# The router's normal rows and constants made beside the first attention, its affine step on ACT, its logits in two banks

## What is computed

```python
x = x + (o @ wo + bo)
hn2 = _layernorm(x, ln2_g, ln2_b).reshape(-1, h)
logits = hn2 @ gate_w + gate_b
idx = jnp.argmax(logits, axis=-1)
mid = jax.nn.relu(jnp.einsum('th,ehf->etf', hn2, w1) + b1[:, None, :])
y = jnp.einsum('etf,efh->eth', mid, w2) + b2[:, None, :]
moe = y[idx, jnp.arange(hn2.shape[0])]
return x + moe.reshape(b, s, h)
```

## Time and profile before

| | us |
|---|---|
| median of three runs | 2004.15 |
| the profiled execution | 2003.47 |
| its span in the trace | 2001.8 |
| first attention, first maxima's product to last residual | 331.27 to 709.41 |
| router, first constant to first load of sorted rows | 710.71 to 779.19 |
| busy over the span: TensorE, VectorE, ACT, POOL | 1750.6, 1582.9, 1286.3, 1103.4 |

### The profile page before, as it was taken

One profiled execution on the slowest core, in us unless ns is written; L12 is line 12 of the kernel. 1 busy time (PEld: TensorE's weight loads), 2 busy tenths in 40 slices (PEclk: granted clock), 3 DMA queues, 4 the chain that ended last, 5 costly groups with the idle time before them and its releaser, 6 DMA issues. The chain is left out here.

```text
span 2001.8 us, 48064 instructions
## 1 busy us (share of the span) xinstructions
PE 1750.6 (87%) x18438; PEld 754.1 (38%) x18438; DVE 1582.9 (79%) x2988; ACT 1286.3 (64%) x2656; POOL 1103.4 (55%) x712
## 2 busy tenths in 40 slices
PE   5537857999999955977999999999999999999997
PEld 3337832233333344653442333333333333333333
DVE  7853567999999565437879999989989899998963
ACT  4503243888888810216884777777887877787785
POOL 8713541000000056331134888989899998989895
PEclk9769977899999956998997999999999999999998
DMA  1230045111111061127994232332323223232311
GB/s 48 36 51 3 1 139 196 49 45 44 49 40 49 13 199 50 50 58 259 373 405 139 69 86 71 80 81 70 86 65 86 75 76 85 66 87 68 82 29 42
DMA packets 194488, 180.14 MB, mean 90 GB/s; under 512 B 58741, under 2 KB 155125, under 8 KB 194053
## 3 DMA queue, kind: packets, MB, share of 16 engines
q1 hardware_dynamic: 185860, 170.01, 29.1%
q0 software_dynamic: 2944, 7.10, 1.1%
q10 hardware_dynamic: 5504, 0.73, 0.2%
HBM read 101.16 MB, written 75.26 MB: 88 GB/s over the span
## 5 line engine op out<-in xcount | busy, mean ns | idle before, releaser
L1037 ACT ACTIVATE probs_l<-exp_l 128x512 f32<-128x512 f32 x1024 | 575.4, 595 | 197.3 <-PE exp_l L1088 189.4
L951 POOL TENSOR_TENSOR part_sums_l<-probs_l 128x1024 f32<-128x1024 f32 x256 | 604.3, 2361 | 110.7 <-ACT probs_l L1037 99.5
L975 DVE TENSOR_REDUCE maxima_l<-max_l 128x1 f32<-128x512 f32 x1024 | 634.0, 682 | 35.5 <-PE max_l L1077 35.5
L1077 PE MATMUL max_l<-k_stack_l,q_stack_l 96*128 96x512 f16 x1024 | 399.7, 391 | 4.0 <-DVE pv_bank_l L967 3.3
L1088 PE MATMUL exp_l<-q_stack_l,k_stack_l 100*128 100x512 f16 x1024 | 390.1, 382 | 5.3 <-ACT probs_l L1037 2.9
L1279 DVE TENSOR_REDUCE maxima_l<-max_l 128x1 f32<-128x512 f32 x512 | 317.1, 683 | 16.6 <-PE max_l L1365 16.5
L1316 ACT ACTIVATE probs_l<-exp_l 128x512 f32<-128x512 f32 x512 | 279.2, 600 | 58.3 <-PE exp_l L1378 54.6
L1122 PE MATMUL pv_bank_l<-probs_l,v_ring_l 128*32 128x512 f32 x2048 | 274.5, 608 | 0.5 <-ACT probs_l L1037 0.5
L1077 PEld LDWEIGHTS max_l<-k_stack_l,q_stack_l 96*128 96x128 f16 x1024 | 100.3, 98 | 328.1 <-DVE maxima_l L975 286.2
L1793 POOL IOTA rows_e<- 128x32 int32 x1 | 0.2, 183 | 384.6 <-POOLq L26 384.6
L957 POOL TENSOR_TENSOR part_sums_l<-part_sums_l 128x512 f32<-128x512 f32 x128 | 163.0, 1273 | 10.0
(11 more groups left out here) (294 smaller groups left out, 2474.8 us busy)
## 6 DMA issues: line engine op xcount, KB each, us to landing
scratch_qk_l<-parts_g SPq DMA_DIRECT2D x128, 256.0 KB, 9.1
q_stack_l<-scratch_qk_l SPq DMA_DIRECT2D x192, 128.0 KB
k_stack_l<-scratch_qk_l SPq DMA_DIRECT2D x192, 128.0 KB
scratch_v_l<-v_g SPq DMA_DIRECT2D x16, 1024.0 KB
v_ring_l<-scratch_v_l SPq DMA_DIRECT2D x64, 256.0 KB, 3.3
scratch_stack_l<-parts_c SPq DMA_DIRECT2D x16, 384.0 KB, 3.8
q_stack_l<-scratch_stack_l SPq DMA_DIRECT2D x64, 96.0 KB, 2.2
k_stack_l<-scratch_stack_l SPq DMA_DIRECT2D x64, 96.0 KB, 2.3
```

Source lines behind the costliest of these rows:

```text
L951: pool.tensor_tensor(part_sums[:, i, h, :, :], probs[:, i, h, 0:2, :], probs[:, i, h, 2:4, :], ALU.add).then_inc(pair_sum.sem, 1)
L975: dve.reduce_max(maxima[:, s % 2, at % NT, at // NT:at // NT + 1], max_bank(n, at)[:, :], AX).then_inc(max_taken.sem, 1)
L1037: act.activation(probs[:, i, at // NT, at % NT, :], exp_ps[at % 2][:, :], ACT.Exp, scale=a.scale).then_inc(prob_tile.sem, 1)
L1077: pe.matmul(max_bank(n, at)[:, :], qs[0:SHIFT_ROW, s % RING, h, k * P:(k + 1) * P], ks[0:SHIFT_ROW, s % RING, h, :], start=True, stop=True ...
```

## The change

- `open_router` allocates the router's rows, constants and gate tensors ahead of `prep_l0`, so that they live through the attention.
- In `attention_l0` SP first issues the four small loads of the gate. POOL makes all constants at the block's start. ACT does, for batch `b` in turn `b + 2`, four sums of 128x128 in group s=1 (one after tile 3, two after tile 9, one after tile 11) and four sums of squares at the same places of group s=2. POOL makes 1/std and the normal rows of the batch from them. This covers batches 0 to 6.
- In `moe` only batch 7 has its moments and normal rows taken as before. The affine step goes from VectorE to ACT. The logits use two banks (those of the experts' first product), so the scores of a batch wait for the choice two before. TensorE transposes two batches ahead and scores one ahead. VectorE's order is: moments 7, choice 0, normal rows 7, destinations 0, choice 1, then choice b and destinations b-1. POOL does one power and then its 32 stores without anything between. ACT does the eight affine steps, then its fills, then the next layer's weights (which stood ahead of the fills).

The core of the diff:

```diff
+ROW_SUMS_AT = {(1, 3): (0,), (1, 9): (1, 2), (1, 11): (3,)}
+ROW_SQUARES_AT = {(2, 3): (0,), (2, 9): (1, 2), (2, 11): (3,)}
...
@@ attention_l0, pool
+            for b in range(ROWS_BESIDE):
+                tiles = slice(b * NT, (b + 1) * NT)
+                pool.wait_ge(row_squared.sem, row_squared.made(b, NT - 1))
+                did(pool.tensor_scalar(rstd[:, tiles], squares[:, tiles], 1.0 / D, None, ALU.mult))
+                settle()
+                did(pool.tensor_scalar(rstd[:, tiles], rstd[:, tiles], LN_EPS, None, ALU.add))
+                settle()
+                did(pool.tensor_tensor(rstd[:, tiles], rstd[:, tiles], g.minus_half[:, 0:NT], ALU.pow))
+                did(pool.tensor_tensor(r.rows[:, tiles, 0:D], g.z[:, tiles, :], bc(minus_mean[:, tiles], D), ALU.add))
+                settle()
+                did(pool.tensor_tensor(r.rows[:, tiles, 0:D], r.rows[:, tiles, 0:D], bc(rstd[:, tiles], D), ALU.mult))
+            settle()
...
@@ attention_l0, act
+            def moments_beside(turn, s, at):
+                b = turn - 2
+                if not 0 <= b < ROWS_BESIDE:
+                    return
+                for k in ROW_SUMS_AT.get((s, at), ()):
+                    tile = b * NT + k
+                    if k == 0:
+
+                        act.wait_ge(y_taken.sem, b + 1)
+                    act.activation(junk[:, k, :], g.z[:, tile, :], ACT.Identity, scale=-1.0 / D,
+                                   accum_out=minus_mean[:, tile:tile + 1]).then_inc(row_summed.sem, 1)
+                for k in ROW_SQUARES_AT.get((s, at), ()):
+                    tile = b * NT + k
+                    act.wait_ge(row_summed.sem, row_summed.made(b, NT - 1))
+                    act.activation(junk[:, k, :], g.z[:, tile, :], ACT.Square, bias=minus_mean[:, tile:tile + 1],
+                                   accum_out=squares[:, tile:tile + 1]).then_inc(row_squared.sem, 1)
...
@@ moe, pool
-            for i in range(B + 2):
-                if i < B:
-                    reciprocal_std(i)
-                if i >= 2:
-                    scatter(i - 2)
+            for b in range(B):
+                scatter(b)
...
@@ moe, vector
-            for i in range(B + 2):
-                if i < B:
-                    take_moments(i)
-                if 1 <= i <= B:
-                    affine(i - 1)
-                if i >= 2:
-                    destine(i - 2)
-                if i < B:
-                    normalise(i)
-                if 1 <= i <= B:
-                    choose(i - 1)
+            take_moments(last_b)
+            choose(0)
+            normalise(last_b)
+            destine(0)
+            choose(1)
+            for b in range(2, B):
+                choose(b)
+                destine(b - 1)
+            destine(B - 1)
             tabulate()
...
@@ moe, scalar
-            act.wait_ge(zeros_ready, 2)
+            for b in range(B):
+                act.wait_ge(zT_ps.sem, zT_ps.made(b, 0))
+                act.activation(hT[:, b % 2, :], zT_bank[b % 2][:, :], ACT.Identity, bias=col[:, 1:2], scale=col[:, 0:1]).then_inc(hT_ready.sem, 1)
+            fill_tails(act, range(E_ // 2, E_))
             act.wait_ge(w_qkv_loaded, 16)
             act.mul(w_qkv[:, :], w_qkv[:, :], W_SCALE).then_inc(w_scaled, 1)
...
@@ moe, tensor
                 pe.wait_ge(hT_ready.sem, hT_ready.made(b, 0))
-                if b:
-                    pe.wait_ge(chosen.sem, chosen.made(b - 1, 0))
+                if b >= 2:
+                    pe.wait_ge(chosen.sem, chosen.made(b - 2, 0))
...
+            transposes(0)
+            transposes(1)
+            score(0)
+            for b in range(B):
+                if b + 2 < B:
+                    transposes(b + 2)
+                if b + 1 < B:
+                    score(b + 1)
+                rank(b)
```

More of the change, by code:

```diff
@@ L1183, with open_router, attention_l0 @@
 L0_OT_AT, L0_OUT_AT = 7, 7
-def attention_l0(nc, g, scratch):
+E_, F_ = 8, 512
+FT = F_ // P
+ROUTES = T + E_
+REGION = B * N + P
+ROW = D + 1
+ROWS_BESIDE = B - 1
+ROW_SUMS_AT = {(1, 3): (0,), (1, 9): (1, 2), (1, 11): (3,)}
+ROW_SQUARES_AT = {(2, 3): (0,), (2, 9): (1, 2), (2, 11): (3,)}
+def open_router(nc, g, ctx):
+    sb = lambda name, shape, dt=F32: ctx.enter_context(nc.sbuf_tensor(name + "_router", shape, dt))
+    r = g.router = Shared()
+    r.gate_w, r.gate_b, r.col = sb("gate_w", [P, E_]), sb("gate_b", [P, E_]), sb("col", [P, 2])
+    r.rows, r.zeros = sb("rows", [P, T, ROW]), sb("zeros", [P, 2 * E_, ROW])
+    r.below, r.ones = sb("below", [P, P]), sb("ones", [P, P])
+    r.pref, r.region, r.upto = sb("pref", [P, NT, E_]), sb("region", [P, E_]), sb("upto", [P, E_, E_])
+    r.steps, r.routes = sb("steps", [P, T]), sb("routes", [P, ROUTES])
+def attention_l0(nc, g, ins, scratch):
     a = L0_ATT
@@ L1202, in attention_l0 @@
         inv_sums, o, oT = sb("inv_sums", [P, NT, HG]), sb("o", [P, NT, U, HG, W]), sb("oT", [P, N])
+        junk = sb("junk", [P, NT, D])
+        minus_mean, squares, rstd = [sb(name, [P, T]) for name in ("minus_mean", "squares", "rstd")]
         cleared = sem("cleared")
@@ L1230, in _ @@
         @block.sync
         def _(sp):
+            sp.dma_start(g.router.gate_w[:, :], ins["L0_ffn_gate_w"]).then_inc(gate_loaded, 16)
+            sp.dma_start(g.router.gate_b[:, :], ins["L0_ffn_gate_b"].partition_broadcast(P)).then_inc(gate_loaded, 16)
+            for n, name in enumerate(("ln2_g", "ln2_b")):
+                sp.dma_start(g.router.col[:, n:n + 1], ins["L0_ffn_" + name].rearrange("(p a) -> p a", a=1)).then_inc(gate_loaded, 16)
             for i in range(2):
@@ L1709, in moe @@
         midT_bank, y_bank = [pb(f"midT{i}") for i in range(2)], [pb(f"y{i}") for i in range(2)]
-        logits_bank, rank_bank = y_bank
+        logits_bank, rank_bank = mid_bank, y_bank[1]
+        r, last_b = g.router, B - 1
         w1, w2 = sb("w1", [P, E_, F_]), sb("w2", [P, E_, FT, D])
         b1, b2 = sb("b1", [P, E_, F_]), sb("b2", [P, E_, D])
[L1713 to L1720, removed]
+        gate_w, gate_b, col, rows, zeros = r.gate_w, r.gate_b, r.col, r.rows, r.zeros
+        below, ones, pref, region, upto, steps, routes = r.below, r.ones, r.pref, r.region, r.upto, r.steps, r.routes
+        stats, mv = sb("stats", [P, NT, 6]), sb("mv", [P, NT, 2])
+        var_eps, rstd = sb("var_eps", [P, NT]), sb("rstd", [P, NT])
         hT = sb("hT", [P, 2, N])
@@ L1791, in _ @@
         def _(pool):
[L1793 to L1815, removed]
+            pool.wait_ge(moments, 1)
+            pool.tensor_tensor(rstd[:, :], var_eps[:, :], g.minus_half[:, 0:NT], ALU.pow).then_inc(rstd_ready, 1)
             def scatter(b):
@@ L1909, in tabulate @@
                 dve.wait_ge(counted, 1)
[L1910 removed]
+                did(dve.tensor_copy(count[:, :], logits_bank[0][:, 0:E_]))
                 settle()
@@ L2032, in rank @@
                 pe.matmul(rank_bank[:, 0:NT * E_], ones[:, :], before[:, at, :], start=False, stop=True).then_inc(rank_ps.sem, 1)
-            for i in range(B + 1):
-                if i >= 1:
-                    score(i - 1)
-                if i < B:
-                    transposes(i)
-                if i >= 1:
-                    rank(i - 1)
-            pe.matmul(logits_bank[:, 0:E_], ones[:, :], before[:, T, :], start=True, stop=True).then_inc(counted, 1)
+            transposes(0)
[7 more added lines that the diff above has]
+                rank(b)
+            pe.matmul(logits_bank[0][:, 0:E_], ones[:, :], before[:, T, :], start=True, stop=True).then_inc(counted, 1)
             pe.wait_ge(experts_in, 64)
```

79 lines of the change are left out of this document (43 added, 36 removed).

## The result

Over four executions the changed kernel took a median of 1986.27 us (1983.01 to 1988.09), the kernel before 2003.31 beside it. The ratio is 0.9906 [0.9894, 0.9919], or 18.8 us off 2003.31 [16.2, 21.2], which puts the changed kernel at 1984.5. The kernel became faster by the forecast's mechanism, and by more than the forecast of 15.2 us: 1984.5 lies 0.5 us under the range's lower end of 1985.0, with an interval of its own from 1982.1 to 1987.1. A repeat gave 0.9904 [0.9890, 0.9917], 1983.8 against 2003.02; one of its six executions took 5528 us, is taken for a slow one and stands in no figure here.

What follows compares the result with a forecast made beforehand. The prediction took POOL's stores to become the router's bound; the router's -15.9 us and the attention drain's +0.7 made -15.2, from 2003.47 to 1988.3 us, with a range of 1985.0 to 1996.5.

Steps and rivals of the forecast that it cites:

- the sum: Whole kernel: router -15.9 us and attention's drain +0.7 make -15.2, from 2003.47 to 1988.3 us.
- The landing: Router's end: from the last store's end to the first load of sorted rows, 1.4 us, at most 5.2.
- The bound: Router: POOL's 32 stores become the bound, with choices running ahead, at a pace of 1.29 us a store.
- Rival 1: Router: stores keep their old pace of 1.47 us, a gain of 10.9 us, 1993.3 in all; chance 0.15.
- The first store: Router's start, built up step by step: first store at 720.3, 7.1 us earlier than 727.39.
- The stores' length: Router: 31 x 1.29 + 1.0 = 41.0 us, plus 0.6 for stores beside big weight loads, 41.6.
- Rival 2: Router's end: another landing is late, 5.2 us behind the last store instead of 1.4, 1992.1; chance 0.06.
- Steady turns at nothing: First attention: ACT's added sums and squares fit its waiting and cost 0 us in the steady turns.
- The drain's 0.7: First attention's last turn: the sums of batch 6 show among ACT's nine exponentials, costing 0.7 us.
- rival 5: Router's start: POOL ends batch 6's rows behind the residual, needing 1.5 us over the upper estimate; chance counted in spread.
- Rival 3: First attention: reads of ACT's accumulators don't overlap, 10.5 us more, 1998.8; chance 0.05.
- Rival 4: First attention: ACT becomes the bound, kernel slower, 2017.6 us; decides from 15.9 us, 2.3 a turn; chance 0.05.

Runs made afterwards that it cites:

- idle powers: Changed kernel with seven unused 128x4 powers put back on POOL, one ahead of each batch's stores but the first; router 59.33 us, 7.1 more.
- the long row: Changed kernel with rows of the sorted table of 640 bytes instead of 516, stored and loaded whole; router 51.74 us, landing 2.07.

## Where the prediction failed, and what of it held

**The step that failed** is the sum, in three of its terms: the router's gain of 15.9 us was made of a first store 10.9 us behind the residual (9.70 measured) and stores of 41.6 us (40.27 measured), each too long, and the attention's drain was charged 0.7 us that it didn't cost. The landing erred the other way (1.4 for 2.22) and hid 0.8 of this, by luck. So the router gave 17.6 us and the attention took nothing, 17.6 together instead of 15.2. The mechanism, POOL's queue as the bound, held.

**The bound.** Right. POOL's stores set the router, with choices running ahead (idle powers: 7.1 us for 7.3). Rival 1, the old pace, is out: 40.27 us for 32 stores, 1.27 apart. The Trainium skill, SBUF — State Buffer, section SBUF: two separate sides, tells of a lock: while a two-port instruction of VectorE runs, POOL can't write its descriptors, which would stretch the stores. Most last 0.95 to 0.96 beside VectorE's small steps; the mean is 963 ns, and 997 with the rows in the router. Little of that difference can be such a lock's: in that run too a store lasts 0.95 to 0.98 unless it is the next behind a power (1.09 to 1.11), but for two of 1.11 and 1.19 near the end that no run explains. Behind the idle powers, with no rows on VectorE, it is 1.04. An estimate from these: the rows on VectorE lengthen five stores by some 0.06, 0.3 us in all.

**The first store.** The mechanism was right, the term too large: 10.9 us behind the residual forecast, 9.70 measured. The clock has no part in this difference: the rows that I took stand at a granted clock of 0.50 (718 to 726 us), as the new start does. Counted from the residual, the transposes of both batches ended at 3.3 us (forecast 3.8; eight took 1.94 on end), the scores of batch 0 at 5.2 (5.7), its choice at 7.3 (7.9) and its rank at 8.5 (9.8). Half a microsecond is the transposes, and 0.7 is at the rank: I had set transposes 2 and scores 1 end to end before it, but each starts as the piece before still runs, its weights being loaded beside, and they kept the rank off only to 718.30, 0.15 behind the choice.

**The stores' length.** 41.6 forecast, 40.27 measured. The mean of before, 0.992, held six stores next behind a power (1.03 to 1.17), of which the change left one, and two long ones near the end; and I added 0.6 for the weight loads besides, though only the first two stores (1.12, 0.98) are longer. The gap between the old pace of 1.47 and 1.29 I had put down to eight powers, which would be 8.3 us over a difference of 31 x 0.18 = 5.6; five stood there, 5.2. The sum doesn't use that reading. At 0.96 and 0.30 it is 31 x 1.26 + 0.96 = 40.0.

**The landing.** 1.4 forecast, 2.22 measured: the likeliest end was too small, since SP's reading of the address was left out, as far as the rows tell. Rival 2's 5.2 is out: the fills had landed.

**The attention.** Steady turns at nothing: right, to 0.01 us. The drain's 0.7 was wrong. ACT around the sums of batch 6, answering to the earlier trace rows:

```profile
691.96 1.59 ACT L1403 ACTIVATE probs_l<-exp_l 128x512 f32<-128x512 f32 x3
693.40 0.34 ACT L1383 ACTIVATE junk_l<-z_res 128x128 f32<-128x128 f32 x1
693.60 0.23 ACT L1383 ACTIVATION_READ_ACCUMULATOR junk_l<-z_res 128x1 f32 x1
693.69 3.07 ACT L1403 ACTIVATE probs_l<-exp_l 128x512 f32<-128x512 f32 x6
696.64 0.32 ACT L1383 ACTIVATE junk_l<-z_res 128x128 f32<-128x128 f32 x1
...
697.23 1.09 ACT L1403 ACTIVATE probs_l<-exp_l 128x512 f32<-128x512 f32 x2
...
705.44 1.04 POOL L1292 TENSOR_TENSOR rows_router<-rows_router,rstd_l 128x512 f32<-128x512 f32 x1
...
710.13 0.69 DVE L1366 TENSOR_TENSOR z_res<-misc_l,z_res 128x512 f32<-128x512 f32 x1 [2.58 <-PE misc_l L1495]
```

The two exponentials behind the gap start at 697.23, 1.41 later than at 695.82, of which 1.4 is the attention's later start. The nine exponentials that the earlier trace rows merges (4.71 us for nine) weren't on end: the third and fourth of them start 0.70 apart, the others 0.48 to 0.50, and the first sum took that place. POOL's rows of batch 6 were done at 706.48, 4.3 us before the residual: rival 5 is out.

**Rival 3**, the reads not overlapping: out, 0.38 us from square to square. No further table load: the attention has one, as before. **Rival 4** was given the right mechanism and the wrong point. Its 15.9 us, 2.3 a turn, treated the slack as one account. It is one for each group, some 1.4 us and what three banks carry, and the change's 1.56 us of squares just fit; twice that costs 0.9 us a turn at full clock, and 11.0 over the attention with what the clock adds.

**What was not priced.** I costed the exchange of the affine step at nothing and the second bank not at all. Undone alone they cost 1.85 and 3.2 us, both through the first two batches. And the 3.45 us of VectorE's wait for the constants, which I read as part of the old start, cost next to nothing when the constants alone went back. That this did no harm is owed to the new start's being built up from its steps and not as old start less parts.

**The range.** Its lower end lay 3.3 us under the forecast, where the terms of the sum were each taken at the likeliest or a cautious value: 1.2 for the start, 1.3 for the stores, 0.7 for the drain, less 0.8 for the landing, 2.4 together. The ratio puts the time another 1.4 lower; in the repeat's trace, where the clock fell later, the router is 1.1 shorter still. The upper side had rivals, the lower had none, though two rows (a mean over mixed surroundings, engines set end to end) could only err to that side.

## What to carry to other kernels

When a stage is bounded by one queue, price the rest of it only until that queue is full: a second bank, or an engine's step moved away, counts during the fill and nowhere later. Slack has to be read in the stretch in which the moved work must end, between the events that hand buffers on, and not as a share of a turn. Work that fills a gap to the last tenth was free here; the same again cost 0.05 us in one group and 0.8 in the next, and only the run could tell.

## What the runs showed of the hardware

**The clock at a stage's edge.** The same instructions of the changed kernel took different time at the router's start. Busy time and granted clock (third figure from the end) in 712 to 716 us, first after, then its repeat:

```profile
712.00:716.00 4.00, 3.83 (x17) 3.46 (x18) 1.42 (x10) 1.56 (x2) 1.02 (x1) 0.50 0.58 149
```
```profile
712.00:716.00 4.00, 3.57 (x24) 3.33 (x23) 2.54 (x17) 2.23 (x3) 1.02 (x1) 0.74 0.70 208
```

At 0.50 TensorE runs at 1.2 GHz, at 1.00 at 2.4. After the change the clock fell at 711.1, ahead of the first product at 712.15; in the repeat only at 713.9, and the first store came 1.24 us earlier (8.46 against 9.70). The eight transposes and the eight first score products took 1.94 and 1.88 us after the change, and in the repeat:

```profile
711.54 1.06 PE L2051 MATMUL zT_ps_e<-ident,rows_router 128*128 128x128 f32 x8 [2.06 <-PEq L26]
713.04 1.10 PE L2059 MATMUL mid_ps_e<-gate_w_router,hT_e 128*128 128x8 f32 x8 [0.43 <-ACT hT_e L2030]
```

In the kernel with the constants in the router the reverse was seen in the attention's drain (the same columns):

```profile
700.00:706.00 6.00, 5.38 (x67) 2.05 (x56) 0.55 (x2) 1.33 (x6) 3.55 (x5) 0.77 0.01 3
```

There the attention was 1.9 us longer (380.63). In the two other kernels with an attention of that length, the rows in the router (380.18) and the long row (380.57), the clock in that window was 0.82 and 0.72; after the change and in its repeat, with 378.7, it was 1.00. In the five kernels whose clock fell in the drain (these three and the two with more steps on ACT) the upper level then lasted into the router, to 2.3 us or more behind the residual; in six of the seven others it fell within 0.6 us of the residual. What decides it isn't shown. It bounds what one profile can tell of a stage that begins or ends with an often idle TensorE: 1.2 to 1.9 us.
